# Rows that carry their gate, adding gathers and fp32 inverses in an attention and experts kernel

## What is computed

```
xn  = layernorm(x)
q, k, v = einsum('bsm,qhdm->bqhsd', xn, W_qkv)        # 16 heads of 64; rotary on 32 of 64 dims of q and k
attn = softmax(where(causal, -inf, q k^T) / 8)
a   = (attn v) W_o
probs = softmax(xn router_w + router_b)               # 8 experts and a ninth "skip" choice
gates = the two largest probs, each at its own choice
y   = sum over the 8 experts e of gates[e] * (gelu(xn w1[e]) w2[e]) + gates[8] * xn
out = x + a + y
```

## Time and profile before

| | |
|---|---|
| median of three runs | 1490.87 us (1490.24 to 1496.87) |
| the profiled execution: its own time | 1500.74 us |
| its span in the profile | 1499.0 us |
| mean granted TensorE clock | 0.965 of full; 1.00 from 200 to 600 us and from 750 to 1400 us, 0.95 from 600 to 700, 0.90 from 700 to 750 |
| busy share: TensorE / VectorE / ScalarE / GpSimd | 84% / 80% / 75% / 57% |
| TensorE weight loads | 63% |

### The profile page before, as it was taken

How to read it: one execution, slowest core, us unless ns; L and a number is a source line. 1 busy time by engine, 2 the same in 40 slices (tenths; PEclk the granted TensorE clock), 3 DMA queues, 4 the chain that set the end, 5 groups by cost and what they waited for, 6 DMA issues and landing times.

```text
span 1499.0 us, 46446 instructions
## 1 busy us (share of the span) xinstructions
PE 1254.0 (84%) x15156; PEld 940.5 (63%) x15157; DVE 1195.7 (80%) x4018; ACT 1122.6 (75%) x3606; POOL 858.6 (57%) x1194
## 2 busy tenths in 40 slices
PE   1416999888888898895999999888888889888888
PEld 1404666666666666664889898566666666666666
DVE  5788877777777887783777777889988889889886
ACT  6415888877787787784878887878777777777786
POOL 3254777777777777773000000767777777666775
PEclk9757999999999999997999999999999999999999
DMA  9621433333333333333232322333333333333330
GB/s 290 204 56 38 101 73 73 74 72 72 74 72 74 72 80 79 75 83 111 72 88 84 87 84 75 77 80 79 80 82 92 91 84 80 89 91 89 85 80 27
DMA packets 115831, 130.12 MB, mean 87 GB/s; under 512 B 11568, under 2 KB 75312, under 8 KB 115376
## 3 DMA queue, kind: packets, MB, share of 16 engines
q1 hardware_dynamic: 107056, 110.26, 30.6%
q0 software_dynamic: 8576, 17.33, 3.8%
HBM read 28.85 MB, written 31.59 MB: 40 GB/s over the span
## 4 chain that ended last, share of the span: by engine, by line
PE 28%; DVE 22%; DMA 17%; POOL 16%; issue 13%; ACT 4%; POOLq 0%; DVEq 0%; SPq 0%; ACTq 0%
DMA sorted_x_dram<-stage,slots 17%; PE bank L1102 6%; PE bank L1103 6%; PE bank L1104 6%; DVE arena L956 4%; POOL sorted_x_dram L497 3%; POOL arena L476 3%; PE bank L1173 3%; DVE arena L919 2%; DVE arena L918 2%; POOL arena L456 2%; PE bank L1184 2%; POOL arena L457 2%; ACT probs L643 2%; PE bank L1211 2%
## 5 line engine op out<-in xcount | busy, mean ns | idle before, releaser
L643 ACT ACTIVATE probs<-arena,neg_max 128x128 f32<-128x128 f32 (+1 forms) x1024 | 452.3, 446 | 110.5 <-DVE neg_max L956 108.5
L956 DVE CUSTOM_DVE_ANT_0 arena<-bank,causal 128x128 f32<-128x128 f32 (+1 forms) x1024 | 302.3, 349 | 46.6 <-PE bank L1173 46.1
L507 POOL DMA_INDIRECT stage<-sorted_y_dram,slots x128 | 130.5, 1020 | 257.9 <-DVE arena L919 238.6
L1184 PE MATMUL bank<-ident,probs 128*128 128x128 f32 x1536 | 212.6, 275 | 13.5 <-ACT probsT L626 10.7
L633 ACT ACTIVATE o_whole<-bank 128x256 f32<-128x256 f32 x256 | 97.7, 382 | 151.5 <-PE bank L1195 85.2
L497 POOL DMA_INDIRECT sorted_x_dram<-stage,slots x128 | 133.3, 1041 | 128.6 <-DMA sorted_x_dram<-stage,slots 104.2
L1184 PEld LDWEIGHTS bank<-ident,probs 128*128 128x128 f32 x1536 | 177.2, 142 | 39.6 <-issue 18.4
L643 ACT ACTIVATION_READ_ACCUMULATOR probs<-arena,neg_max 128x1 f32 x1024 | 194.7, 190 | 0.0
L1102 PE MATMUL bank<-arena 128*128 (+1 forms) x864 | 183.2, 238 | 1.5 <-DVE arena L1076 1.5
L476 POOL TENSOR_TENSOR arena<-o_whole,arena 128x256 f16<-128x256 f32 x256 | 172.0, 672 | 21.0
L1103 PE MATMUL bank<-arena 128*128 (+1 forms) x864 | 182.7, 238 | 0.0
(11 more groups left out here) (152 smaller groups left out, 3258.8 us busy)
## 6 DMA issues: line engine op xcount, KB each, us to landing
arena<-arena SPq DMA_DIRECT2D x256, 256.0 KB, 3.8
arena<-sorted_x_dram SPq DMA_DIRECT2D x72, 128.0 KB, 2.2
sorted_y_dram<-stage SPq DMA_DIRECT2D x72, 128.0 KB, 1.8
sorted_x_dram<-arena SPq DMA_DIRECT2D x3, 2304.0 KB, 17.8
arena<-experts_dram SPq DMA_DIRECT2D x8, 512.0 KB, 5.6
out_dram<-acc SPq DMA_DIRECT2D x32, 128.0 KB
sorted_x_dram<-arena SPq DMA_DIRECT2D x1, 2368.0 KB, 19.1
sorted_x_dram<-stage,slots POOLq DMA_INDIRECT x128, 2.5
```

Source lines behind the costliest of these rows:

```text
L643: last = nc.scalar.activation(probs[:, s % 4, at:at + w], masked[:, s % 4, at:at + w], ACT.Exp, bias=neg_max[:, s % 4, t:t + 1], scale=-1. ...
L956: last = nc.vector.tensor_tensor_reduce(out=masked[:, (s + i) % 4, at:at + w], in0=SC[i][:, at:at + w], in1=causal[:, at:at + w], scale=1. ...
L1184: last = nc.tensor.transpose(TP[s % 2][:, k * P:(k + 1) * P], probs[:, s % 4, k * P:(k + 1) * P], ident[:])
```

## The change

**Rows carry their gate.** Sorted rows are 129 floats: 128 of the row and its gate. GpSimd copies the gate column into the stage buffer before each send; there are two stage buffers, not four. Expert tiles are loaded with the column.

**Weighting beside the experts.** GpSimd multiplies each expert result by the gate column (`gate`), two instructions a tile, before SyncE stores it. SyncE now loads tile i+4 after that store. ScalarE, in period 0 of sample 16, waits for the last stores.

**Gathers add.** `gather` is an indirect DMA with an add into the row of `acc`; `combine` is gone. The order of the four gathers of a pair of tiles is tile 0, tile 1, tile 0, tile 1.

**Inverses as fp32.** `invert` is one reciprocal a pair, one period earlier; `turn_sums` is four fp32 matmuls against the fp32 identity, done just ahead of the transposes in the period of its `attend`.

**Three output buffers.** `o_copy` waits for the value products and for the split of three outputs ago.

**Unit plan.** "rest 0" of sample b+2 moves from period 5 to period 3 (not in samples 0 and 16), and the sort that put "rest" last in its period is gone.

```diff
-AHEAD = ((5, "rest", 0), (6, "rope", 0), (7, "rest", 1))
+AHEAD = ((3, "rest", 0), (6, "rope", 0), (7, "rest", 1))
+AHEAD_OPENING = ((5, "rest", 0), (6, "rope", 0), (7, "rest", 1))
-T_LAG, PV_LAG, OUT_LAG, INV_LAG, SPLIT_LAG, BACK_LAG = 1, 2, 2, 3, 4, 2
+T_LAG, PV_LAG, OUT_LAG, COPY_LAG, SPLIT_LAG = 1, 2, 2, 3, 4
+BACK = ((0, 0), (1, 0), (0, 1), (1, 1))
-    return sorted(steps, key=lambda step: (step[0], step[1] == "rest" or step[0] == 6 and step[1] == "v_low"))
+    return sorted(steps, key=lambda step: step[0])
...
-        stage = sb("stage", [P, BACKS, D], F32)
+        stage = sb("stage", [P, SENDS, ROW], F32)
...
+        sent_rows = nc.dram_tensor("sent_rows_dram", (ROWS, ROW), F32, kind="Internal").ap()
...
                 for k in range(BODY):
                     i = BODY * n + k
-                    if not last:
-                        sp.wait_ge(xs_ready, i + 1)
-                        load(i + BODY, k)
-                    sp.wait_ge(y2_done, i + 1)
+                    sp.wait_ge(gated, i + 1)
...
                     sp.dma_start(rows.rearrange("(k p) d -> p k d", p=P), ys[k % 2]).then_inc(ys_out[k % 2], 16)
+                    if not last:
+                        load(i + BODY, k)
...
+                nc.gpsimd.tensor_copy(stage[:, i % SENDS, D:ROW], gates[:, tile, 0:1]).then_inc(send_ready, 1)
...
-                pool.wait_ge(send_ready, tile + 1)
                 pool.wait_ge(sent, 16 * (TOP * tile + n))
+                if n > 0:
+                    nc.gpsimd.tensor_copy(stage[:, i % SENDS, D:ROW], gates[:, tile, n:n + 1]).then_inc(send_ready, 1)
+                pool.wait_ge(send_ready, TOP * tile + n + 1)
+                pool.wait_ge(normalised, tile + 1)
...
+            def gate(i, k):
+                pool.wait_ge(y2_done, i + 1)
+                for j in range(ET // P):
+                    last = nc.gpsimd.tensor_scalar(ys[k % 2][:, j, :], ys[k % 2][:, j, :], xs[k][:, j, D:ROW], 1.0, ALU.mult, ALU.mult)
+                last.then_inc(gated, 1)
...
-                if not (u == 0 and k < BACKS):
-                    pool.wait_ge(combined, TOP * PER * u + k - BACKS + 1)
+                t, n = BACK[k % 4]
+                tile = (TPS * u if k < 4 else TPS * b) + t
+                if n > 0:
+                    pool.wait_ge(gathered[t], 32 * u + 16 * (k // 4) + 16)
+                elif k >= 4:
+                    pool.wait_ge(mixed, b + 1)
                 nc.gpsimd.indirect_dma_start(
-                    out=stage[:, k % BACKS, :], out_offset=None, in_=sorted_y[0:ROWS, :],
+                    out=acc[:, tile, :], out_offset=None, in_=sorted_y[0:ROWS, :], compute_op=ALU.add,
...
-                act.wait_ge(inv_turned, J + 1)
-                if not (isinstance(J, int) and J < 2):
-                    act.wait_ge(o_done, J - 1)
+                act.wait_ge(pv_done, 2 * J + 2)
+                if J >= OUTPUTS:
+                    act.wait_ge(o_done, J - OUTPUTS + 1)
...
+            def invert(J):
+                dve.wait_ge(exp_done, 2 * J + 2)
+                if J >= 2:
+                    dve.wait_ge(inv_turned, J - 1)
+                of = slice(J % 2 * 2, J % 2 * 2 + 2)
+                nc.vector.reciprocal(inv_total[:, of, :], total[:, of, :]).then_inc(inv_done, 1)
...
+            def turn_sums(b, j, at):
+                pe.wait_ge(inv_done, 8 * b + j + 1)
...
+                    pe.wait_ge(o_scaled, 8 * b + j - 1)
+                for t in range(TPS):
+                    for i in range(2):
+                        of = inv_total[:, j % 2 * 2 + i, t:t + 1].broadcast_to([P, DK])
+                        last = mm(INV[j % 2][64 * i:64 * i + 64, t * P:(t + 1) * P], of, ident[:], start=True, stop=True)
+                last.then_inc(inv_turned, 1)
```

More of the change, by code:

```diff
@@ L35 @@
 BITS = E.bit_length() - 1
-BACKS = 4
+ROW = D + 1
+SENDS = 2
+OUTPUTS = 3
 LC = 16
@@ L537, in _ @@
             rest_of(MID - 1)
+            for i in range(TILES):
+                gate(i, i % BODY)
             for done in ys_out:
@@ L657, in sample @@
                         exps(b, s, at == OPENING)
+                    if at == REOPEN and p == 0:
+                        for done in ys_out:
+                            act.wait_ge(done, 16 * TILES // 2)
                     for kind, j, of, u, psum in units_at(b, p):
@@ L885, in row @@
                 return v[:, tile, :] if isinstance(tile, int) else v[:, bass.ds(tile, 1), :].rearrange("p a d -> p (a d)")
[L887 to L898 removed]
             def mix(b):
                 if b < MID:
[L903 removed]
+                    dve.wait_ge(normalised, TPS * b + TPS)
                 for t in range(TPS):
@@ L1030, in sample @@
                             mix(b - 1)
-                    then = past(b, p, BACK_LAG)
-                    if then and b >= MID:
-                        combine(*then)
                     for kind, j, of, u, psum in units_at(b, p):
@@ L1043, in rest_of @@
                     mix(b)
-                else:
-                    for k in range(PAIRS - BACK_LAG, PAIRS):
-                        combine(b, k)
                 o_scale(8 * b + 7, 7)
```

158 lines of the change are left out of this document (61 added, 97 removed).

## The result

The changed kernel takes 1694.48 us (median of four runs, 1690.02 to 1700.43), against 1491.68 for the kernel before beside it: a ratio of 1.1355, 95% interval 1.1304 to 1.1406. The forecast was slower, 1563 us, with a range that ended at 1604. So the sign was right and the size wrong: +203 us instead of +72.

The account below looks back on a forecast made before the run. Bounds: GpSimd and its scatters in former samples, TensorE in expert tiles, VectorE and TensorE alternating in latter samples. Terms 59 + 18 - 5 = +72 us took the 1490.9 us median to 1563, range 1515 to 1604.

Parts of the forecast that it names:

- Expert tiles, +59: Expert stage: loads issued behind the gated store come 1.7 us late, 0.86 us a tile over 68 tiles, +59 us.
- The new wait is 2.0 + 2.6 - 1.8 = 2.8 us, about the whole 2.3 won: Latter samples: the wait for the q stacks eats the gain, so 13 of 16 samples stay at about 35.3 us.
- the ring: Moved "rest 0": ScalarE's copy waits for all four q stacks, then VectorE's low part frees the y unit's bank; 2.8 us.
- TensorE alone would need 33.0, and up to 2.3 us a sample can be won: Latter samples: with VectorE relieved, TensorE's own work would set 33.0 us a sample instead of 35.3.
- In the former samples the same ring lies just inside GpSimd's loop: 0: Former samples: the wait for the q stacks is hidden by GpSimd's loop and costs 0.
- Sends with gates, +18: Former samples: gate-column copies and 516-byte rows cost 1.1 us a sample, +18 us (-8 to +45).
- The turn, +0.21 a period: TensorE, latter samples: the fp32 turn takes 0.43 instead of 0.21 us, 1.7 us a sample; hidden in former samples.
- Gathers, 0: Latter samples: adding gathers take GpSimd about 1.04 us to twice that to issue, which its free time covers; 0.
- VectorE's relief, 6.5 us a sample: Latter samples: VectorE loses eight combines and four inverts, gains eight reciprocals; 6.5 us less work a sample.
- The first: Rival: the q-stack wait doesn't bite, latter samples fall to 33.0 us, total 1533; chance 0.17.
- The second: Rival: GpSimd held up more, by adding gathers at 2 us or more or gates excluded by VectorE; 1595; chance 0.12.
- The third and fourth: Rivals with expert loads hidden: VectorE's relief decides, 1474, chance 0.08; or q stacks eat it, 1490 to 1497, chance 0.04.

Follow-up runs that it names:

- third experiment: Changed kernel with the load of tile i+4 issued early again, GpSimd copying each gate column to a small buffer: 1635.8 us.
- first experiment: Changed kernel with the old unit plan and the old order within a period put back: 1588.12 us, ratio 1.0511.
- kernel 10: Changed kernel with old plan, early loads, two output buffers, four staged rows, plain gathers, half-precision turn, gates out of the rows: 1504.48 us.
- fourteenth kernel: Changed kernel with old plan and early loads, plus the turn ahead of the period's units: 1504.8 us, ratio 1.0054.
- thirteenth: The twelfth kernel with the inverses and their turn in fp32 again: 1463.67 us, ratio 0.9782.
- twelfth kernel: kernel 10 with the turn of the inverses ahead of the period's units on TensorE: 1494.94 us.
- kernel 8: Changed kernel with old plan, early loads, two output buffers and four staged rows, gathers still adding: 1525.76 us.
- kernel 7: kernel 8 with gathers that don't add, VectorE adding the fetched rows: 1509.54 us.

## Why the prediction was wrong in size

**Expert tiles, +59: right.** Measured +64.2, by the links and in the place that it gave, and the third experiment takes it away whole. The clock, too, was nearly full there as forecast (0.98). Its upper end, +83 by the Trainium skill (SBUF — State Buffer, "Who interferes with whom"), was not reached: the gates ran at 0.375 us each and the chain above has no wait ahead of them. But only 13 of the 144 gate passes overlapped one of VectorE's two-input passes (L1074) by 0.1 us or more (0.39 us in the median, the others 0.37), so the rule was hardly put to the test.

**"The new wait is 2.0 + 2.6 - 1.8 = 2.8 us, about the whole 2.3 won": the step that failed, in the latter samples.** The mechanism was the right one, with the right engines in it, and the wait was nearly the right length. What failed is what the sum made of it. TensorE's products of the y units say how long it waited for the ring (the kernel after, then the first experiment):

```profile
L1100 PE MATMUL bank<-wvo_lo,arena 128*128 128x128 f16 x512 | 110.2, 247 | 104.3 <-DVE arena L933 99.6 <-POOL arena L479 4.7
...
L1100 PE MATMUL bank<-wvo_lo,arena 128*128 128x128 f16 x512 | 94.1, 226 | 30.8 <-POOL arena L479 30.8
```

99.6 us over the 27 samples that have the moved step and a y unit behind it (1 to 14 and 17 to 29, counted from 0), the usual ones: by TensorE's timeline 3.4 us in each of the 13 latter ones (3.1 to 4.3) and 3.9 in each of the 14 former ones. With the plan back there is no such wait; the 30.8 us there are waits for GpSimd's split. The ring costs more than that, 67 us of the latter stage (628.3 against 561.0), or 5.2 a usual sample, because of the clock. Behind the stall the granted clock was low; two period 4s with the same 60 products show its price (the stall of sample 23, the stretch behind it, then the whole period of sample 26 and that of sample 23; columns as above):

```profile
1352.50:1357.50 5.00, 0.71 (x15) 0.38 (x12) 0.73 (x2) 1.35 (x3) 3.75 (x4) 0.77 0.56 132
1357.50:1361.50 4.00, 3.98 (x33) 3.46 (x34) 2.36 (x12) 2.64 (x11) 2.23 (x3) 0.50 0.22 28
...
1475.86:1483.34 7.48, 4.31 (x60) 3.28 (x59) 3.55 (x14) 4.48 (x14) 5.61 (x7) 1.00 0.38 78
1352.55:1363.24 10.69, 6.38 (x60) 5.10 (x59) 3.64 (x14) 4.48 (x14) 6.73 (x7) 0.68 0.51 98
```

In sample 26 the clock stayed full: 4.31 us of work and 3.17 of waiting. In sample 23 it fell to 0.50, 1.2 GHz, during a wait of 4.31 us, and the same work took 6.38. The clock stayed full in 4 of the 27 usual samples and fell in the other 23. Over the 13 latter ones TensorE's work in period 4 took 6.06 us in the mean, with the plan back 4.25. So the 67 us are some 45 of waiting and some 24 at the lower clock. The forecast carried 13 x 2.3 = 30 for the ring and had no term for the clock. The clock followed the stalls and was no cause of its own: with them gone it was full again.

The landing was misread: the 3.8 us in the earlier trace rows were those of the first stack of the four, the only one whose landing the trace gave. In the kernel before, the DMA engines still moved 148 GB/s from 1128.5 to 1129.0 and nothing from 1129.5 on, so the fourth stack, put down as landed at 1128.4, was still on its way then. In the kernel after the fourth landed 5.1 to 6.3 us after its issue in the usual latter samples. The wait was longer than forecast by less than this; probably TensorE itself came later to the y unit than the forecast had it, which wasn't measured.

The other half of the miss lies under the ring: **"TensorE alone would need 33.0, and up to 2.3 us a sample can be won"**. Without the ring a latter sample takes 35.04 us, not 33.0, some 33 us in all: of the 2.0 a sample, 1.2 are the place of the turn and 0.9 the adding gathers (both below).

**"In the former samples the same ring lies just inside GpSimd's loop: 0": the step that failed, in the former samples.** It had no working: the ring there was never added up. Putting the plan back took 34 us off (600.0 to 565.6), with early loads 47 (609.5 to 562.5); in the kernel before, the plan alone put 56 on (593.2 against 537.3). TensorE waited 3.9 us a sample for the ring, and its work in period 4 took 5.8 us, with the plan back 4.5; part of this took the place of waits that were there already. By how much the ring overran GpSimd's loop isn't shown.

**Sends with gates, +18: right, as far as can be told.** Taking the gates out of the rows took 18 us off the former stage, which varies by up to 10, and 21 off the total. Without the ring (first experiment) the former stage was 28 us above the one before. The Trainium skill (DMA: Bandwidth & Descriptors, "How a descriptor splits into AXI transactions") would have made it 31; the sends landed in 2.4 us in the median, before in 2.5, so nothing of that rule shows in them. In kind it does show in the clears: with rows of 516 bytes instead of 512 they took 32.4 and 34.4 us to land where they took 17.8 and 19.1, and in kernel 10, with 512 again, 17.8 and 18.9. Their 0 held all the same: the first sample starts at 114.67 us, before at 114.78.

**The turn, +0.21 a period: right as far as it went.** fp32 itself costs 0.24 (4.21 against 3.97, and 4.06 against 3.82). Not seen was that the diff also moves the turn from ahead of the units to behind them, 0.15 a period, 1.2 a sample; the fourteenth kernel gives the total for it, 18 us, of which a part is period 1.

**Gathers, 0: wrong.** The issue time of 1.585 us lay within the ends given (1.04 to 2.08), and GpSimd had the room; but what follows it slows, on VectorE too, and that is 0.9 us a latter sample, 14 us of the latter stage and 16 of the total.

**The third output buffer, 0: right** within what can be told. **VectorE's relief, 6.5 us a sample: real but smaller**: VectorE was busy 31.7 us in a latter sample before, 26.4 after and 26.1 in the first experiment. Two small instructions fewer a pair, which are a part of it, are worth 31 us once nothing stands ahead of them (thirteenth against twelfth kernel), 21 of them in the latter stage.

In sum: of 203 us the plan made 106 and the loads 59, measured singly and together 172. The 31 that are left are the turn's place (18), the gates in the rows (18 to 21) and the adding gathers (16), less what VectorE's relief gives; those were measured in other kernels each, and what the relief gives in this one wasn't measured, so the 31 aren't closed.

**The rivals.** The first (the wait doesn't bite) was out: it bit in all 27 usual samples. The second had a true part, a dearer gather (1.6 us, not 2), and missed that VectorE's mix pays for it. The third and fourth needed hidden loads. The range missed because its top, 1604, took in the upper ends of the expert and former terms alone: the +1.0 a latter sample stayed out of it (some 13 us), and the ring in the former samples and the clock had no upper end at all.

## What to carry to other kernels

When a copy is moved ahead of the transfers that read its buffer, add up the ring for every stage that it runs in, with the landing of the last transfer of a burst, not of the first; the same step cost nothing in period 4 and 106 us in period 3. Give a stall of TensorE a term for the clock behind it: here 3.4 us of waiting came with 1.8 us of slower work. A step that reads a last column of a buffer keeps the whole buffer: copy the column out and the load needn't wait. And a diff that changes an instruction may also move it: of the turn's 0.39 us a period, 0.15 was the move.

## What the runs showed of the hardware

- Four SBUF-to-SBUF transfers of 256 KB in a burst (the kernel after, the sample shown): the first landed 3.8 us after its issue, the third 6.5, the fourth 6.3. Over the 13 usual latter samples the fourth took 5.1 to 6.3.
- An indirect gather that adds took GpSimd 1.585 us to issue, one that doesn't 1.02; the software queue has 22912 packets with the adding ones and 8576 with plain ones, all else alike (kernels 8 and 7).
- In the sample shown TensorE did nothing for 4.3 us, and its granted clock was 0.50 in the 4 us of work behind it. Waits of 3.1 to 5.9 us came with a lower clock in 23 of the 27 usual samples; in the other 4 (3.2 to 3.6 us) it stayed full.
- Rows of 516 instead of 512 bytes nearly doubled the landing of a clear (17.8 to 32.4 us; 17.8 again in kernel 10) and left that of a scatter of 128 rows as it was (2.5 and 2.4).
- Behind an adding gather the passes of GpSimd took 0.94 instead of 0.73 us and VectorE's mix beside them 2.68 instead of 1.39. In the mean over 400 us of latter samples a mix instruction took 1.31 us in kernel 8 and 0.74 in kernel 7.
